# A fused eight-layer kernel, second attention stage: scores two steps ahead, and ScalarE's exponentials of the next step ahead of its copy of this step's turned probabilities

## The reference

```python
def _attn(q, k, v):
    s = jnp.einsum('bhqd,bhkd->bhqk', q, k) * SCALE
    p = jax.nn.softmax(s, axis=-1)
    return jnp.einsum('bhqk,bhkd->bhqd', p, v)
```

## Time and profile before

| | |
|---|---|
| median of 3 runs | 1137.84 us (1134.45 to 1142.14) |
| the profiled execution | 1136.88 us |
| its span, from the first to the last instruction | 1135.6 us |
| TensorE busy | 949.6 us, 84% of the span |
| VectorE busy | 730.4 us, 64% |
| ScalarE busy | 519.2 us, 46% |
| GpSimd busy | 300.4 us, 26% |
| TensorE's share of the chain that ended last | 59% |
| VectorE's share of it | 15% |
| mean granted clock of TensorE | 0.925 |

### The profile page before, as it was taken

One profiled execution on the slowest core, in us unless ns is written; L12 is line 12 of the kernel. 1 busy time (PEld: TensorE's weight loads), 2 busy tenths in 40 slices (PEclk: granted clock), 3 DMA queues, 4 the chain that ended last, 5 costly groups with the idle time before them and its releaser, 6 DMA issues.

```text
span 1135.6 us, 14899 instructions
## 1 busy us (share of the span) xinstructions
PE 949.6 (84%) x4834; PEld 679.5 (60%) x4834; DVE 730.4 (64%) x1864; ACT 519.2 (46%) x1330; POOL 300.4 (26%) x281
## 2 busy tenths in 40 slices
PE   5677679999999999999997798865878788976556
PEld 2222234668999998888975576733545555544445
DVE  5899994335666668687665346557677855567653
ACT  3574461136666665665632343443356542132331
POOL 3477791131111112143105204341222100010110
PEclk9887899999999999999999799987789999989678
DMA  8400001011111172113004246220100003211100
GB/s 313 201 1 0 1 0 46 1 42 29 43 43 33 43 260 98 43 63 100 11 20 168 74 139 195 94 89 15 43 1 1 1 2 134 74 40 38 70 19 19
DMA packets 28356, 73.96 MB, mean 65 GB/s; under 512 B 4076, under 2 KB 5366, under 8 KB 27640
## 3 DMA queue, kind: packets, MB, share of 16 engines
q1 hardware_dynamic: 24344, 63.28, 16.2%
q0 software_dynamic: 3072, 8.39, 2.3%
q10 hardware_dynamic: 864, 1.34, 0.3%
HBM read 50.98 MB, written 22.02 MB: 64 GB/s over the span
## 4 chain that ended last, share of the span: by engine, by line
PE 59%; DVE 15%; ACT 3%; issue 3%; another core or an unknown queue 2%; POOL 1%; SPq 1%; DMA 1%; DVEq 0%; POOLq 0%; ACTq 0%
PE psum L2042 5%; PE psum L946 5%; PE psum L1652 4%; PE psum L1138 4%; PE psum L1149 4%; PE psum L807 4%; PE psum L1118 4%; PE psum L949 3%; PE psum L1666 2%; PE psum L1129 2%; DVE arena L2338 2%; PE psum L818 2%; PE psum L970 2%; PE psum L2061 2%
## 5 line engine op out<-in xcount | busy, mean ns | idle before, releaser
L1028 POOL TENSOR_TENSOR arena<-arena,mhalf 128x8 f32<-128x8 f32 x32 | 53.7, 1678 | 258.5 <-DVE arena L1013 258.5
L1250 DVE SCALAR_TENSOR_TENSOR X<-psum,arena,X 128x256 f32<-128x256 f32 x128 | 55.9, 478 | 66.7 <-PE psum L1149 64.5
L418 POOL TENSOR_TENSOR arena<-arena 128x512 f32<-128x512 f32 x64 | 83.5, 1331 | 7.4 <-DVE arena L735 4.2
L735 DVE TENSOR_TENSOR_SCAN arena<-psum,arena 128x512 f32<-128x512 f32 x64 | 74.6, 1207 | 3.3 <-ACT psum L610 1.8
L1192 ACT ACTIVATE arena<-psum,arena 128x256 f32<-128x256 f32 x128 | 60.0, 477 | 34.9 <-DVE arena L1229 34.7
L481 PE MATMUL psum<-arena,ident 128*128 128x512 f32 x128 | 72.3, 690 | 1.1 <-POOL arena L418 0.8
L1652 PE MATMUL psum<-arena 128*128 x248 | 66.4, 391 | 7.4 <-DVE arena L1747 4.0
L1758 DVE COPY arena<-psum 128x256 f32<-128x256 f32 x62 | 26.2, 422 | 64.5 <-PE psum L1666 55.3
L1149 PE MATMUL psum<-arena 128*128 128x256 f32 x256 | 65.9, 380 | 1.2 <-DVE X L1250 1.1
L1138 PE MATMUL psum<-arena 128*128 128x256 f32 x256 | 66.5, 383 | 0.0
L2323 ACT ACTIVATE arena<-psum,arena 128x240 f32<-128x240 f32 x128 | 57.4, 465 | 19.1 <-DVE arena L2343 14.6
(11 more groups left out here) (348 smaller groups left out, 2282.5 us busy)
## 6 DMA issues: line engine op xcount, KB each, us to landing
arena<-in_w SPq DMA_DIRECT2D x32, 384.0 KB
tokens<-arena SPq DMA_DIRECT2D x2, 4096.0 KB, 23.0
arena<-tokens SPq DMA_DIRECT2D x32, 256.0 KB
results<-arena SPq DMA_DIRECT2D x32, 256.0 KB
arena<-in_moe SPq DMA_DIRECT2D x17, 384.0 KB, 3.0
arena<-in_moe SPq DMA_DIRECT2D x4, 1536.0 KB, 13.8
arena<-in_w SPq DMA_DIRECT2D x2, 1024.0 KB, 6.6
arena<-in_gu SPq DMA_DIRECT2D x1, 1280.0 KB, 5.9
```

What stands on the lines that cost most here:

```text
L418: nc.gpsimd.tensor_tensor(m.HC[:, v, :], m.Hs[:, v, :], m.Cs[:, s % 2, :], ALU.mult).then_inc(*tick("HC", s, c))
L735: nc.vector.tensor_tensor_scan(m.Hs[:, 2 * (s % 2) + c, :], bank[m.bank_dA[c]], input_of(m, s, c), 0.0, ALU.mult, ALU.add).then_inc(*tick( ...
L1250: a = nc.vector.scalar_tensor_tensor(k.X[:, t, :], bank[5][:, j * D:(j + 1) * D], m.ri[:, u % 4, j:j + 1], k.X[:, t, :], ALU.mult, ALU.add)
```

## The change

In the loop, TensorE gives the scores of step s + 2 after the transposes of s, where it gave those of s + 1 ahead of them. VectorE makes the maxima of s + 2 after its copy of s, where it made those of s + 1 at the start of the step. ScalarE makes the exponentials of s + 1 ahead of its copy of s, where it made them after it. The hand-over from the stage before gives the scores and the maxima of steps 0 and 1, where it gave those of step 0; ScalarE's hand-over is unchanged. Number, kind and size of all instructions stay as they were. In the changed kernel, ScalarE's copy is on L2752, VectorE's sum and copy on L2805 and L2811.

```diff
@@ attention2_pe @@
     for s in range(B * STEPS):
         b, g = s // STEPS, s % STEPS
-        if s + 1 < B * STEPS:
-            a2_scores_pe(k, m, s + 1)
         transposed(s)
+        if s + 2 < B * STEPS:
+            a2_scores_pe(k, m, s + 2)
         if b and g == 0:
             turned(b - 1)
@@ attention2_act @@
         b, g, u = s // STEPS, s % STEPS, s % 2
+        if s + 1 < B * STEPS:
+            a2_exponentials_act(k, m, s + 1)
         act.wait_ge(*at("a2_T", s, 0))
         if s >= 2:
             act.wait_ge(*at("a2_AV", s - 2))
         nc.scalar.copy(m.PT[:, 2 * u, :, :], bank[4].rearrange("p (t d) -> p t d", t=2)).then_inc(*tick("a2_PTa", s))
-        if s + 1 < B * STEPS:
-            a2_exponentials_act(k, m, s + 1)
@@ attention2_dve @@
         b, g, u = s // STEPS, s % STEPS, s % 2
-        if s + 1 < B * STEPS:
-            a2_maxima_dve(k, m, s + 1)
         if b < B - 1 and g in (4, 7):
             a2_fetch_dve(k, m, b + 1, g // 7)
         dve.wait_ge(*at("a2_E", s))
...
                               bank[5].rearrange("p (t d) -> p t d", t=2)).then_inc(*tick("a2_PTv", s))
+        if s + 2 < B * STEPS:
+            a2_maxima_dve(k, m, s + 2)
         if b and g == 0:
             normalised(b - 1)
@@ tensor_program @@
-              lambda: a2_scores_pe(k, a2, 0))
+              lambda: (a2_scores_pe(k, a2, 0), a2_scores_pe(k, a2, 1)))
@@ vector_program @@
-               lambda: a2_maxima_dve(k, a2, 0))
+               lambda: (a2_maxima_dve(k, a2, 0), a2_maxima_dve(k, a2, 1)))
```

## The result

| | before | changed |
|---|---|---|
| median | 1138.03 us | 1133.12 us |
| lowest to highest, 20 runs each | 1134.45 to 1142.80 | 1128.58 to 1136.49 |
| ratio, 95% interval | | 0.9948 [0.9936, 0.9960] |
| the profiled execution | 1136.88 us | 1133.62 us |
| its span | 1135.6 us | 1132.3 us |

The change wins 5 us, 0.5%. That is less than the 1% named as the bound of no change, though its interval is clear of zero, and it is under a third of the forecast 17 us. The direction and the range (1112 to 1136) held; the size did not.

A forecast was written before the change was run, and what follows sets the result against it. Plain steps were taken as bound by TensorE's work, steps 0 to 7 by VectorE, with gains in irregular steps: 2.1 + 5.8 + 5.5 + 4.9 = 18.3 us, less 1.3, 17.0, giving 1121 us; range 1112 to 1136.

The forecast's parts named there:

- The three waits of the projection: Last three stretches: TensorE's output projection waits 4.1 us for bank 5 from VectorE's copy; all of it was to go.
- that term: Steps 0 to 7: scores of step 9 fill the 3.43 us wait for values of step 7, winning 1.1 us.
- the term for the third stretch: Steps 8 to 15: earlier turning of keys and queries and filled waits win 5.8 us, bounds 2.6 and 8.75.
- 2.1 + 5.8 us: Gains forecast for the first two batches: 2.1 us in steps 0 to 7 and 5.8 us in the third stretch.
- the slower rival: ScalarE's copy behind late exponentials costs TensorE 0.48 us in each of eleven places: +5 us, 1143 us; chance 0.08.
- I leave 0.65 for that: Fourth stretch, a batch's third step: 0.65 us left for the output's transposes waiting for bank 4 behind exponentials and copy.
- the slack of 0.4 us: Plain steps: some 4.1 us of TensorE work cover 3.7 us of maxima, exponentials and ScalarE's copy, leaving 0.4 us.
- The fourth stretch: Steps 16 to 23: 5.5 us to be won of 7.2 us of TensorE idle time, bounds 2 and 7.2.
- the fifth: Steps 24 to 31: 4.9 us to be won, 0.9 us of clock regained included, bounds 2 and 6.8.
- Scores and maxima of step 4 can now be done ahead of this stop: Steps 0 to 7: 1.82 us of VectorE work moves ahead of its 7.10 us stop, 1.0 us left after later gathers.
- the clock's 5.4 us: Rival: filling TensorE's idle gaps also lifts its lowered clock, 5.4 us more, 1115.5 us; chance 0.10.
- VectorE's dependencies, at 1129: Rival: only 8.6 us of waits for VectorE's copy vanish, waits for exponentials stay; 1129 us, chance 0.22.

The follow-up runs named there:

- the experiment above: Against the kernel before: scores and maxima two steps ahead as in the change, ScalarE's copy ahead of the next exponentials as before; 1095.24 us, 0.9893.
- the correction: Changed kernel, but ScalarE copies first at the third step of batches 1 to 3; 1092.43 us, 0.9895 of the kernel before.
- both corrections: Changed kernel with old steps 0 to 7 and hand-over, and ScalarE's copy first at third steps; 1125.09 us, 0.9877 with stops; 1090.44, 0.9848 without.

## Why the prediction was wrong

**Right.** The three waits of the projection are gone, plain steps do not grow (3.08 us), scores follow the transposes without a wait of their own, and the first gather came 0.9 us later after the first scores (0.8 forecast). The 3.3 us ahead of the turning of keys and queries fell to 0.8. At the end of step 7 the wait ahead of the values fell from 3.43 to 2.15 us, which is the 1.1 us of that term. What the term for the third stretch said, 5.8 us, the trace gave: 41.1 to 35.5 us for the second batch from one L2690 to the next. That is in part luck: the third step's wait in it was 2.14 us where 0.7 was left, and the first batch grew by as much as this one shrank. In the two pairs of traces with stops the first two batches together took 119.6 and 118.1 us before and 119.7 and 119.1 changed, where 2.1 + 5.8 us were forecast to go. The condition of the slower rival, exponentials that end late, decided just where it held: alone on ScalarE the order costs 1.4%. One reading of the earlier trace rows was too simple: the plain step of 3.25 us was taken as TensorE's work with 0.11 us of idle time, but the same ring over ScalarE's copy and exponentials sets it as in the experiment above, and without the ring it is 3.08 us.

**The step that failed: "I leave 0.65 for that"**, the wait ahead of the output's transposes at a batch's third step. The prediction saw that "TensorE asks for bank 4 early" there, and worked the price out from exponentials that start with the transposes: 2.04 + 0.59 us against 2.1. They started 1.75 us after these (867.01 against 865.26), and 2.3 us in the two other batches, because at this step VectorE brings the bias late. So the mechanism was right and the size wrong: 2.1, 2.4 and 2.1 us in place of 0.7, 0.65 and 0.65, 4.6 us more, and the values behind each ran at a lower rate, 1.84, 1.92 and 1.57 us in place of 1.06, another 2.2. Undone, it gives 6.5 us. The rows of before showed what was needed: the slack of 0.4 us had been worked out for plain steps alone, while GpSimd's and VectorE's extra work falls in the second and third step of a batch. In the kernel before, step 18's bias subtraction was already stretched to 0.65 us, and its transposes waited 1.38 us for exponentials:

```profile
864.19 0.65 DVE L2343 TENSOR_SCALAR arena<-arena 128x2 f32<-128x2 f32 x1
...
866.07 1.09 PE L2662 MATMUL psum<-ident,arena 128*128 128x128 f32 x8 [1.38 <-ACT arena L2325]
```

The fourth stretch (5.5 forecast) gave 2.8 us by its L2690s, the fifth (4.9) gave 3.5. With the correction the same two, on other chips, take 32.9 and 26.4 us where the kernel before took 38.7 and 32.7: 5.8 and 6.3 us. The idle time that the two terms counted on was there to be had.

**The second that failed: "Scores and maxima of step 4 can now be done ahead of this stop".** The first stop hit VectorE ahead of step 2's copy, and the maxima of step 4 then stood behind the second one and ahead of what TensorE wanted. "1.82 us of VectorE's work are gone from a stretch that VectorE bounds" was false as well: over the batch no work goes (168 operations either way in the two traces without stops), and the filling between VectorE's copies goes. The 2.1 us forecast were -4.0 in the profile, and the order costs 2.6 to 2.7 us where there are no stops. That the stops make it worse is what the traces suggest (the first batch, by its L2690, 5.7 and 7.9 us longer in two pairs, the second 5.6 and 6.9 us shorter), and the times do not settle it: on the chip with the stops both corrections together gave 6.9 us, no more than the 9.1 on the chip without.

Rivals: the clock's 5.4 us do not show, 0.91, 0.95 and 0.95 being granted in the last three batches where it was 0.92, 1.00 and 0.95, with half-rate pieces behind the new waits; VectorE's dependencies, at 1129, come nearest in time, but not as a cause: the waits for exponentials that it kept are gone.

With both steps as the prediction had them, the changed kernel becomes the one with both corrections: 13.1 us on the chip with stops, 16.7 and 13.5 on the others, near the forecast's 17. What was wrong was that the change as made has them. On the chip that the forecast was for, the nearest of these is 13.1, so some 4 us of it are missing even then. By the traces they are missing in the first two batches, which took 115.4 us with both corrections, against 119.6 and 118.1 in the two of the kernel before: 4.3 and 2.7 us, where 2.1 + 5.8 were forecast. That is the part in which the stops fall; how much they take of it was not measured.

## What to carry to other kernels

Look-ahead and the order on the consuming engine are two edits: time them apart. Here scores two steps ahead win 1.1%. Moving long exponentials ahead of a short copy takes 0.2 us off a plain step in the traces, less than the times can resolve, and costs 6.5 us at three places. Before putting an operation that may be late ahead of a ready one that another engine wants soon, find the steps where it is late (those with extra work on whoever feeds it) and work out the price there, not in the plain step. In a stretch that one engine bounds, keep work between its copies that needs no one: in the first batch the order that puts each copy right behind its transposes had it wait for them 6.2 us, and cost 2.7 us. And a step in which one engine looks full may be a ring over two engines that is only a little longer than its work, as the 3.26 us here against 3.08: follow it round once before calling it that engine's.

## What was not expected of the hardware

The same kernel took 1138 us on some chips and 1106 to 1107 us on others. In the six traces of the slower ones VectorE stands for 11.6 to 15.1 us in this stage, up to 10.8 us at a time, while GpSimd gathers or shortly after, and ScalarE up to 12.4 us at a time; the profile names no releaser of its own ("remote"). On the others this stage shows no such stop. The place at which it hits moves from one execution to the next. The changed kernel, traced on one chip of each kind (spans of 1132.3 and 1098.1 us), shows where the 34 us lie: the stage begins 17.4 us later, where "remote" stops stand too, its first batch is 16.7 us longer, and everything behind it is equal within 0.2 us. What the stops are was not found.

VectorE's subtraction on 128x2 elements, 0.17 us in the earlier trace rows, took 1.12 us while GpSimd ran an operation of 1.27 us beside it: a small operation can be stretched by several times. It adds 0.95 us to the delay that TensorE meets two engines further on; in the two other batches it added 0.3 us, and TensorE waited nearly as long.
